# The same calls of four engines in another order, in a cross-attention and mixture FFN kernel

## The reference

```python
x = x + xattn(layernorm(x), ctx)          # x: 16 x 112 x 256, ctx: 16 x 375 x 256
x = x + ffn(layernorm(x))
# xattn: q, k, v = t@Wq+bq, c@Wk+bk, c@Wv+bv; softmax(q k / 16) v
# ffn, over 8 experts e:
#   h_e   = silu(x @ w_gate[e]) * (x @ w_up[e])      # 256 -> 1024
#   out   = sum_e cw_e * (h_e @ w_down[e])           # 1024 -> 256
#   cw    = softmax(x @ w_router) * softmax(10 * x @ w_gating), normalised over e
```

## Time and profile before

| | |
|---|---|
| median of 3 runs | 940.03 us |
| profiled execution | 939.91 us, of which 938.1 us are its span and 1.8 us lie around it |
| 448-column passes in a row, from 173.58 to 912.08 us | 3598 |
| 938.1 us by stage | 0 to 90: attention; 90 to 142: plain quads; 142 to 190: `opening`; then 13 x `four`, of some 52 us each; 870 to 924: `closing`; the last rows |
| ScalarE, VectorE, GpSimd busy | 77, 79, 82% |
| granted TensorE clock | 1.00 to the last slice |

### The profile page before, as it was taken

One profiled execution on the slowest core, in us unless ns is written; L12 is line 12 of the kernel. 1 busy time (PEld: TensorE's weight loads), 2 busy tenths in 40 slices (PEclk: granted clock), 3 DMA queues, 4 the chain that ended last, 5 costly groups with the idle time before them and its releaser, 6 DMA issues.

```text
span 938.1 us, 16160 instructions
## 1 busy us (share of the span) xinstructions
PE 932.3 (99%) x4923; PEld 856.5 (91%) x4923; DVE 740.9 (79%) x1416; ACT 720.2 (77%) x1431; POOL 772.7 (82%) x690
## 2 busy tenths in 40 slices
PE   9999999999999999999999999999999999999998
PEld 7999898999999999999999999999999999999998
DVE  4998447777888888888888888888888888888774
ACT  7988555778887788878788877888787888878761
POOL 5899976788889796978788897969787887969655
PEclk9999999999999999999999999999999999999999
DMA  8463422121201110010101110110201120111126
GB/s 218 127 162 82 115 78 87 40 85 43 65 24 45 43 65 24 15 64 10 65 23 46 44 65 23 38 50 2 80 8 46 43 65 23 46 43 45 38 40 157
DMA packets 73244, 55.94 MB, mean 60 GB/s; under 512 B 30244, under 2 KB 69485, under 8 KB 73158
## 3 DMA queue, kind: packets, MB, share of 16 engines
q1 hardware_dynamic: 73150, 54.91, 20.2%
q10 hardware_dynamic: 8, 0.00, 0.0%
HBM read 46.58 MB, written 6.48 MB: 57 GB/s over the span
## 4 chain that ended last, share of the span: by engine, by line
PE 97%; DVE 1%; ACT 1%; issue 1%; POOL 0%; DVEq 0%; ACTq 0%
PE ps L419 94%; PE ps L2588 1%; DVE xf L1940 0%; PE ps L2624 0%; PE ps L2686 0%; PE ps L2576 0%; PE ps L2641 0%; DVE early L1860 0%; POOL xc_lo L716 0%; ACT w_hi L1175 0%; PE ps L2534 0%; ACT arena L1069 0%; PE ps L2667 0%; ACT xc_hi L1151 0%; ACT xf L1077 0%
## 5 line engine op out<-in xcount | busy, mean ns | idle before, releaser
L419 PE MATMUL ps<-xc_hi,w_hi 128*128 128x448 f32 x904 | 332.3, 368 | 1.4 <-ACT shared L1336 1.4
L419 PE MATMUL ps<-xc_hi,w_lo 128*128 128x448 f32 x904 | 331.6, 367 | 0.0
L419 PE MATMUL ps<-xc_lo,w_hi 128*128 128x448 f32 x904 | 331.5, 367 | 0.0
L419 PE MATMUL ps<-arena 128*128 128x448 f32 (+5 forms) x1588 | 307.4, 332 | 0.2 <-DVE arena L430 0.2
L419 PEld LDWEIGHTS ps<-arena 128*128 128x128 f32 (+2 forms) x1588 | 254.1, 186 | 16.4 <-DVE arena L430 0.4
L763 POOL TENSOR_TENSOR arena<-shared,arena 128x448 fp32r<-128x448 f32 x168 | 193.5, 1162 | 21.1 <-ACT arena L1387 17.2
L419 PEld LDWEIGHTS ps<-xc_hi,w_hi 128*128 128x128 f32 x904 | 169.7, 188 | 17.8 <-ACT shared L1336 1.8
L419 PEld LDWEIGHTS ps<-xc_hi,w_lo 128*128 128x128 f32 x904 | 169.7, 188 | 15.8
L419 PEld LDWEIGHTS ps<-xc_lo,w_hi 128*128 128x128 f32 x904 | 169.8, 188 | 14.8
L430 DVE TENSOR_TENSOR arena<-ps,arena 128x448 fp32r<-128x448 f32 (+2 forms) x126 | 79.5, 635 | 41.9 <-ACT arena L1232 20.1
L752 POOL TENSOR_TENSOR w_lo<-w_raw,w_hi 128x1792 fp32r<-128x1792 f32 (+1 forms) x17 | 66.1, 3886 | 46.6 <-ACT w_hi L1185 46.6
(11 more groups left out here) (217 smaller groups left out, 1775.5 us busy)
## 6 DMA issues: line engine op xcount, KB each, us to landing
early<-in_L_ffn_w_down SPq DMA_DIRECT2D x16, 512.0 KB, 3.8
xf<-cw_dram SPq DMA_DIRECT2D x16, 448.0 KB, 4.6
shared<-in_ctx SPq DMA_DIRECT2D x16, 336.0 KB
w_raw<-in_L_ffn_w_gate SPq DMA_DIRECT2D x17, 256.0 KB, 2.7
w_raw<-in_L_ffn_w_up SPq DMA_DIRECT2D x17, 256.0 KB, 3.2
early<-in_L_ffn_w_gate SPq DMA_DIRECT2D x15, 256.0 KB, 2.7
early<-in_L_ffn_w_up SPq DMA_DIRECT2D x15, 256.0 KB, 3.0
xsacc<-in_x SPq DMA_DIRECT2D x8, 224.0 KB, 6.5
```

What stands on the lines that cost most here:

```text
L419: ins = nc.tensor.matmul(dst, w, m, start=first and i == 0, stop=last and i == len(passes) - 1, skip_group_check=onto)
```

## The change

No call is added or taken out, and the functions called are the same; the lists `opening`, `four` and `closing` of TensorE, ScalarE, VectorE and GpSimd are put in another order. Some calls move over the border of one `four` into the one before (TensorE's `up_3(m - 1)` and `down_4(g - 1)`, VectorE's `weigh(g - 1, 3)` and `add_up(g - 1, 3)`, GpSimd's two `low_hidden(m - 1, ...)` and a `sum_of_set`), and `opening` and `closing` with them. SyncE's list is unchanged. TensorE's `four`, and the part of ScalarE's that goes with its first two quads:

```diff
 # TensorE, four(m): the order before, and after it the order of the change
-gate_1(m), up_3(m-1), up_4(m-1), up_1(m), down_4(g-1), gate_5(m), gate_6(m), gate_2(m),
-up_6(m), up_2(m), down_1(g), gate_7(m), gate_3(m), up_7(m), down_2(g), up_5(m), down_6(g),
-up_3(m), up_4(m), down_7(g), gate_4(m), gate_1(m+1), gate_5(m+1), up_1(m+1), gate_6(m+1),
-gate_2(m+1), down_5(g), up_6(m+1), gate_7(m+1), up_2(m+1), down_3(g), up_7(m+1), up_5(m+1),
-gate_3(m+1), gate_4(m+1), up_3(m+1), down_4(g), up_4(m+1), gate_1(m+2), up_1(m+2),
-gate_5(m+2), gate_6(m+2), gate_2(m+2), up_6(m+2), gate_7(m+2), gate_3(m+2), up_2(m+2),
-up_7(m+2), down_1(g+1), gate_4(m+2), gate_1(m+3), up_5(m+2), down_2(g+1), up_3(m+2),
-down_6(g+1), gate_5(m+3), up_4(m+2), up_1(m+3), down_7(g+1), gate_6(m+3), gate_2(m+3),
-down_5(g+1), up_6(m+3), gate_7(m+3), down_3(g+1), up_2(m+3), up_7(m+3), up_5(m+3),
-gate_3(m+3), gate_4(m+3)
+gate_1(m), up_4(m-1), up_1(m), gate_5(m), gate_6(m), gate_2(m), down_1(g), up_6(m), up_2(m),
+gate_7(m), gate_3(m), down_2(g), gate_4(m), up_7(m), up_5(m), down_6(g), up_3(m),
+gate_1(m+1), gate_5(m+1), down_7(g), up_4(m), up_1(m+1), down_5(g), gate_6(m+1), up_6(m+1),
+down_3(g), gate_2(m+1), up_2(m+1), gate_7(m+1), up_7(m+1), gate_3(m+1), up_5(m+1),
+down_4(g), up_3(m+1), gate_4(m+1), gate_1(m+2), up_4(m+1), up_1(m+2), gate_5(m+2),
+gate_6(m+2), gate_2(m+2), up_6(m+2), up_2(m+2), gate_7(m+2), down_1(g+1), gate_3(m+2),
+up_7(m+2), down_2(g+1), gate_4(m+2), up_5(m+2), down_6(g+1), up_3(m+2), gate_1(m+3),
+gate_5(m+3), up_4(m+2), down_7(g+1), up_1(m+3), down_5(g+1), gate_6(m+3), up_6(m+3),
+down_3(g+1), gate_2(m+3), up_2(m+3), gate_7(m+3), up_7(m+3), up_5(m+3), gate_3(m+3),
+down_4(g+1), up_3(m+3), gate_4(m+3)
 # ScalarE, around gate_seed(m+1)
-activate21(m), high_hidden(m, HID11), gate_seed(m+1), high_hidden(m, HID22), high_t3(m), up_seed(m+1)
+activate21(m), high_hidden(m, HID11), high_hidden(m, HID22), gate_seed(m+1), gate_keep5(m+1), high_t3(m), up_seed(m+1)
...
 # TensorE, opening (m = 4, g = 1), up to its last row product
-gate_1(m), up_1(m), turn_cw(), gate_5(m), ... up_5(m), down(g, 0), gate_1(m+1), up_3(m), down(g, 1), gate_5(m+1), up_4(m), up_1(m+1), ... up_3(m+1), down(g, 5), down(g, 6), up_4(m+1)
+gate_1(m), gate_5(m), up_1(m), gate_6(m), ... up_5(m), down(g, 0), up_3(m), down(g, 1), up_4(m), gate_1(m+1), up_1(m+1), ... down(g, 5), up_5(m+1), down(g, 6), up_3(m+1)
...
```

More of the change, by code:

```diff
@@ L952, in four @@
                 low_t1(m + 2)
[L954 to L989, removed]
+                low_hidden(m + 3, HID11, g11, 0, 0)
+                low_hidden(m + 3, HID22, g22[1], 1, TC)
             def closing():
@@ L3057, in four @@
                 gate_2(m)
+                down_1(g)
                 up_6(m)
                 up_2(m)
+                gate_7(m)
+                gate_3(m)
+                down_2(g)
+                gate_4(m)
+                up_7(m)
+                up_5(m)
+                down_6(g)
+                up_3(m)
+                gate_1(m + 1)
+                gate_5(m + 1)
+                down_7(g)
+                up_4(m)
+                up_1(m + 1)
+                down_5(g)
+                gate_6(m + 1)
@@ new lines, in four @@
+                up_6(m + 1)
+                down_3(g)
+                gate_2(m + 1)
+                up_2(m + 1)
+                gate_7(m + 1)
+                up_7(m + 1)
+                gate_3(m + 1)
+                up_5(m + 1)
+                down_4(g)
+                up_3(m + 1)
+                gate_4(m + 1)
+                gate_1(m + 2)
+                up_4(m + 1)
+                up_1(m + 2)
+                gate_5(m + 2)
+                gate_6(m + 2)
+                gate_2(m + 2)
@@ new lines, in four @@
+                up_6(m + 2)
+                up_2(m + 2)
+                gate_7(m + 2)
+                down_1(g + 1)
+                gate_3(m + 2)
+                up_7(m + 2)
+                down_2(g + 1)
+                gate_4(m + 2)
+                up_5(m + 2)
+                down_6(g + 1)
+                up_3(m + 2)
+                gate_1(m + 3)
+                gate_5(m + 3)
+                up_4(m + 2)
+                down_7(g + 1)
+                up_1(m + 3)
+                down_5(g + 1)
@@ L3060, in four, with closing @@
+            def closing():
+                m = QUADS - CP * FPAIRS
+                g, hn = m // FPAIRS - 1, m // (CP * FPAIRS)
+                gate_1(m)
+                up_4(m - 1)
+                up_1(m)
+                gate_5(m)
+                gate_6(m)
+                gate_2(m)
                 down_1(g)
@@ L3062, in four @@
                 gate_3(m)
+                up_6(m)
+                up_2(m)
+                gate_4(m)
                 up_7(m)
                 down_2(g)
+                down_6(g)
                 up_5(m)
[L3066 to L3070 removed]
                 gate_1(m + 1)
                 gate_5(m + 1)
+                up_3(m)
+                down_7(g)
+                up_4(m)
+                down_5(g)
+                gate_6(m + 1)
                 up_1(m + 1)
[L3074 removed]
+                down_3(g)
                 gate_2(m + 1)
[L3076 removed]
+                gate_7(m + 1)
                 up_6(m + 1)
[L3078 removed]
+                gate_3(m + 1)
                 up_2(m + 1)
[L3080 removed]
                 up_7(m + 1)
                 up_5(m + 1)
[L3083 removed]
                 gate_4(m + 1)
+                down_4(g)
                 up_3(m + 1)
[L3086 removed]
                 up_4(m + 1)
```

859 lines of the change are left out of this document (410 added, 449 removed).

## The result

The changed kernel takes 943.41 us (median of 7 runs, 941.55 to 943.86), the kernel before 939.69 in the same comparison (7 runs, 938.24 to 941.69). The ratio of the means is 1.0031, its 95% interval 1.0017 to 1.0046: a small loss, but clear of no change. The forecast was 930.1 and the range 929.0 to 944.0: the time lies inside it, but on the other side of no change, at the rival called slow for good (943.0 to 943.5).

What follows compares the result with a forecast made beforehand. TensorE was taken to bound the kernel, at one of two paces. Profiled 939.91 - 9.4 (fast throughout) - 0.4 (`opening`) - 0.1 (`down_4(27)`) = 930.0, put at 930.1 us for the median; range 929.0 to 944.0.

Steps and rivals of the forecast that it cites:

- slow for good: Rival: the second down_3, at 219 us, leaves slow and nothing ends it; 943.0 to 943.5 us, chance 0.32.
- What bounds it: 448-column passes, 173.58 to 912.08 us: TensorE bounds, at two paces, PEld 90.9% (206.7 ns) or 92.6% (202.7 ns).
- The late loads: 26 loads, nearly all gate_6 or gate_7, 10 to 68 ns late, can change pace; new order has none; taken as 0 us.
- The need of 50 ns: At gate_6(29): a load wants its signal 50 ns ahead; the tightest new waits leave 0.277 to 0.301 us.
- The places: down_3: where it begins in the beat of five decides the pace; 120 passes between visits keep the place; fast throughout.
- place 0: The 199 gap in the fast beat 199, 207, 202, 203, 202; down_3 begun there stays fast, leaving at place 1.
- The single loads of `ident_cw`: down_3's second and fifth passes: each load's effect, read by place, was combined to predict place 1 leaving fast at place 3.
- the fast one: Main case, fast throughout: slow stretches' 456.42 us of loads at 92.59%, 9.4 us less; 930.1 us, chance 0.50.
- The price of slow for good: Fast stretches from the second down_3, 218.8 us, run at the slow pace: 3.6 us more.
- `opening`: TensorE's 1.43 us wait on up_keep5(4) goes, waits of 0.4 and 0.8 us for VectorE come; bounds -1.7 to +1.7, taken -0.4.
- The 64-deep window: Rival, late signal does not matter: the window hides a signal 20 ns late, time stays at 940; no separate chance.
- The gap of 189.2 ns: Same rival, by the gap formula: 3598 passes freed of waits come at 189.2 ns, saving 58 us; 882 us, chance 0.01.

Runs made afterwards that it cites:

- three passes: Changed kernel, ident_cw where it had been, with three more passes of 448 columns ahead of gate_1(7) in TensorE's opening: 931.34 us, ratio 0.9881 to the kernel before.
- The kernel before with the tile moved: The kernel before, order untouched, with the tile ident_cw starting 448 bytes later in SBUF: 933.81 us, ratio 0.9919.
- the kernel with 448 bytes: The changed kernel with the tile ident_cw starting 448 bytes later in SBUF: 930.76 us, ratio 0.9889 to the kernel before.

## Why the prediction was wrong

**What bounds it: right.** Two paces at one clock, told apart by PEld's share and not by the busy time of PE or the clock, and a sum that is the share times the stretch.

**The late loads: right.** None is left, and a late load can turn the pace in both directions and costs next to nothing itself; both are now shown and not only read off. The need of 50 ns was 50 to 53. One of the 26 loads, at `down_4(27)`, was 209 ns late and not 10 to 68; it changes nothing in the sum.

**The places: the step that failed.** That 120 passes keep the place, and that the first `down_3` begins at place 0 and the second at place 1, came true. Misread was that the fast beat begins behind every row product: in the trace of before one more stretch behind a row product, at 164.39 us, begins 210, 206, 207. The stretch that matters did start fast. Wrong was: "In that pass the clock phase is that of place 4, from which it would come out fast at place 3, and 3 stays 3. That is the nearest row, and I go by it, without much trust". The single loads of `ident_cw` do not add up so: the second one, met in the middle of 205, 205, 202, made it 204, 205, 205, 201 and slow. A row for that meeting was not in the trace, and I let a guess about a phase carry half of all chances where its two outcomes were 13 us apart. With place 1 open the slow case deserved at least as much as the fast one: all 16 visits in the slow pace and both at place 4 left slow, and a place can only be kept for good where it leads to itself, which one of five was seen to do. The rule was good enough to find the fix: three passes would have been named by it.

**The price of slow for good: right.** Forecast 3.6 us from the second `down_3` on; measured 3.22 + 0.24.

**`opening`: mis-sized, and its cause misread.** Forecast -0.4, measured -1.65 us. The wait went and neither 0.4 nor 0.8 us came in its place. My laying out gave 0.6 us too much in `opening` before; taking that off would have given -1.0, still short. Nor had `up_keep5(4)` stood behind a copy of a weight set. The rows of the kernel before have it behind an `activate` that waited 3.38 us for VectorE's `gate_c12`, and VectorE was held up by `sums_2_4`, a subtraction of 448 columns that took 4.47 us while GpSimd's `low_set` ran:

```profile
148.55 4.47 DVE L1940 TENSOR_TENSOR xf<-xf 128x448 f32<-128x448 f32 x1 [0.27 <-POOL xc_lo L716]
148.47 4.07 POOL L752 TENSOR_TENSOR w_lo<-w_raw,w_hi 128x1792 fp32r<-128x1792 f32 x1
154.67 0.58 ACT L1373 ACTIVATE shared<-shared 128x448 f32<-128x448 f32 x1 [3.38 <-DVE shared L1979]
155.16 0.51 ACT L1336 COPY shared<-ps 128x448 f32<-128x448 f32 x1
```

In the changed kernel the same subtraction begins before that `low_set` and takes 0.62 us:

```profile
149.92 0.62 DVE L1940 TENSOR_TENSOR xf<-xf 128x448 f32<-128x448 f32 x1
```

The kernel before with the tile moved shows it as before does (4.46 us). I had laid out the new queues with durations of this trace, and that may be where the waits of 0.4 and 0.8 us for VectorE came from. That the overlap with GpSimd's instruction is what stretches it was not tested.

**The rivals.** Slow for good (0.32) was what happened. Its sum with the measured `opening`, 939.91 + 3.5 - 1.65, is the profiled 941.8. That the median falls into 943.0 to 943.5 is partly luck: `opening` gave 1.25 us more than that sum had, and the median lies 1.6 us above the profiled execution. The 64-deep window of the Trainium skill (TensorE: Matmul & The Clock Gate, section "Back-to-back issue gap") did not hide a signal that came late: one 34 ns ahead, 18 short of the 52, moved its load by 18 ns. The gap of 189.2 ns for 448 columns comes from a formula that this section of the Trainium skill gives for an isolated matmul; of a stream of loads and matmuls the section says that both set the distance, so the rival used the formula where the section does not. The measurement decides: as a steady distance 189.2 appeared in no kernel of this study; the fast pace stays at 202.7 with no late load and no disturbance in 3595 passes.

**What the fast pace gives back.** Forecast 9.4 us of gain with it. From pass 1242 to the last `down_3` the kernel with 448 bytes takes 686.43 us where the kernel before took 695.62: 9.2 of them. At the start of the last product pass it is 12.3 us ahead of the changed kernel (924.73 and 937.04 us), at the end of the span 10.9. Its last chain does not end on TensorE. GpSimd's seven last sums and VectorE's very last one, of the changed kernel and then of that one:

```profile
932.28 4.93 POOL L912 TENSOR_TENSOR w_raw<-w_raw,xsacc 128x256 f32<-128x256 f32 x7 [2.96 <-DMA xsacc<-xsacc]
...
937.36 0.48 DVE L2028 SCALAR_TENSOR_TENSOR w_raw<-ps,cw,w_raw 128x256 f32<-128x256 f32 x1 [0.26 <-PE ps L419]
```

```profile
921.49 4.88 POOL L912 TENSOR_TENSOR w_raw<-w_raw,xsacc 128x256 f32<-128x256 f32 x7 [4.48 <-DMA xsacc<-xsacc]
...
926.47 0.48 DVE L2028 SCALAR_TENSOR_TENSOR w_raw<-ps,cw,w_raw 128x256 f32<-128x256 f32 x1 [0.20 <-POOL w_raw L912]
```

VectorE's last sum is released by TensorE in the one and by GpSimd in the other, and GpSimd had begun when a DMA had landed (10.8 us earlier, where TensorE is 12.3 us earlier). That DMA is the next thing to move; it wasn't tried. The two orders with the tile moved (933.81 and 930.76 us) differ in their traces by 1.6 us in `opening`, 2.8 from there to the last `down_3`, and 1.4 the other way behind it (the rest is the attention).

## What to carry to other kernels

When TensorE is 100% busy, look at the share of its weight loads by windows; where it takes two values, list the starts in nanoseconds around each border and look for two things: a load that began late, and a tile whose start has another remainder of 256 bytes than the others. Put every stationary tile of a loop at one remainder and every streamed tile too (here both had the same one); that was worth 0.8% in the one order here (933.81 against 941.25 us) and, by the two ratios to the kernel before, 1.4% in the other (0.9889 against 1.0031). The order of calls still matters through its late loads (933.81 against 930.76 us). Before a wait is put down to the call ahead of it, look at what that call itself waited for. Where an order is periodic, one small shift decides for all rounds: a step whose outcome no row shows deserves even chances, not the nearest row's.

## What the runs showed of the hardware

- Steady passes of 448 columns keep one of two paces at the same granted clock of 1.00 (its upper level, 2.4 GHz): 202.67 ns in a beat of five, or 206.67 ns. In these traces nothing but a late load, a wait, a pass of another length or a tile at another remainder moved it from one to the other.
- Loads of a weight tile that started 64 or 128 bytes off the others' remainder of 256 shifted the beat (943.41 and 930.86 us); with it 256 bytes off, or at the others' remainder of 512, they did not (930.49 and 930.76 us). A streamed tile at 320 past a multiple of 512 among tiles at 128 and 384 shifted it too (937.68 us, and 931.68 with it at 384). Why was not found.
- The first load of `up_3` began 50 to 53 ns after the end of the ScalarE copy that it waits for, where that was later than its turn (25 cases).
- A subtraction of 448 columns on VectorE took 4.47 and 4.46 us in the two kernels where a GpSimd subtraction of 1792 columns ran beside it, and 0.62 us in the kernels where it did not.
